# Out-projection issued group by group into a bank of its own, with two banks left for transposes and routing

## What is computed

```python
q = rope(einsum("bim,ghmd->bghid", x, w_aq)); k = rope(einsum("bim,gmd->bgid", x, w_ak))
v = einsum("bim,gmd->bgid", x, w_av)
s = einsum("bghid,bgjd->bghij", q * D**-0.25, k * D**-0.25) - 1e30 * (i < j)
o = einsum("bghij,bgjd->bghid", softmax(s), v)
r = einsum("bghid,ghdm->bim", o, w_ao)            # the out-projection
x1 = layernorm(x + r)
out = layernorm(x1 + routed_experts(x1) + shared_expert(x1))
```

## Time and profile before

| | us |
|---|---|
| median of 3 runs | 1107.93 |
| profiled execution, its own time | 1108.6 |
| its span, first to last instruction | 1106.8 |
| TensorE busy, share of the span | 1000.8 (90%) |
| VectorE | 654.8 (59%) |
| ScalarE | 523.8 (47%) |
| GpSimd | 370.4 (33%) |

### The profile page before, as it was taken

The page is one execution under the profiler, slowest core; times in us unless marked ns, Lnnn a source line. Parts: engine busy times, 40 slices in busy tenths (PEclk is TensorE's granted clock), DMA queues, the critical chain, the costliest instruction groups (busy, mean ns, idle before and its releaser), DMA issues.

```text
span 1106.8 us, 17288 instructions
## 1 busy us (share of the span) xinstructions
PE 1000.8 (90%) x5448; PEld 756.0 (68%) x5448; DVE 654.8 (59%) x1666; ACT 523.8 (47%) x1151; POOL 370.4 (33%) x407
## 2 busy tenths in 40 slices
PE   6999999699999999999998999999999998639826
PEld 4888887566778777777676666777777776526502
DVE  6777765366565576565655775564757647324408
ACT  4333334454564556464654555555655645116502
POOL 6666666223321212102134333212221120126722
PEclk9999999899999999999998999999999999859958
DMA  8455333533231212210223323432211123998697
GB/s 242 165 180 186 106 138 116 180 110 118 78 96 62 59 58 58 70 44 23 86 64 112 103 82 103 126 110 66 78 35 58 36 59 107 226 245 208 94 277 277
DMA packets 107417, 128.36 MB, mean 116 GB/s; under 512 B 16465, under 2 KB 73925, under 8 KB 107328
## 3 DMA queue, kind: packets, MB, share of 16 engines
q1 hardware_dynamic: 84688, 96.82, 28.4%
q10 hardware_dynamic: 13408, 22.09, 6.5%
q0 software_dynamic: 9232, 8.34, 4.2%
HBM read 81.99 MB, written 58.59 MB: 127 GB/s over the span
## 4 chain that ended last, share of the span: by engine, by line
PE 71%; DVE 12%; issue 6%; DMA 4%; ACT 2%; POOL 2%; SPq 1%; ACTq 0%; DVEq 0%; POOLq 0%
PE s_ps L1051 15%; PE o_ps L1078 11%; PE ring L1061 9%; PE ring L1090 9%; PE o_ps L1081 6%; PE s_ps L1022 5%; PE ring L1022 5%; DVE neg_max L1253 2%; PE s_ps L1144 2%; PE s_ps L1029 1%; PE s_ps L1054 1%; DVE fsum L1452 1%; PE ring L1105 1%; DVE pt_lo L1191 1%; ACT pt_hi L830 1%
## 5 line engine op out<-in xcount | busy, mean ns | idle before, releaser
L1253 DVE TENSOR_REDUCE neg_max<-s_ps 128x1 f32<-128x128 f32 (+7 forms) x256 | 191.7, 751 | 165.1 <-PE s_ps L1054 160.9
L1051 PE MATMUL s_ps<-kt,qt_hi 128*128 128x512 f32 (+3 forms) x768 | 243.9, 399 | 8.4 <-POOL qt_lo L776 6.1
L904 ACT ACTIVATE probs<-s_ps,neg_max 128x128 f32<-128x128 f32 (+7 forms) x256 | 189.4, 740 | 130.6 <-DVE neg_max L1253 122.9
L776 POOL TENSOR_TENSOR qt_lo<-q_raw,qt_hi 128x512 fp32r<-128x512 f32 x64 | 81.9, 1281 | 325.3 <-ACT qt_hi L830 325.1
L1061 PE MATMUL ring<-ident,probs 128*128 128x128 f32 x1152 | 176.8, 276 | 7.2 <-DVE pt_lo L1191 4.5
L1051 PEld LDWEIGHTS s_ps<-kt,qt_hi 128*128 128x128 f32 x768 | 139.3, 194 | 64.3 <-issue 37.9
L1078 PE MATMUL o_ps<-pt,v 128*128 128x512 f32 x336 | 174.0, 600 | 2.7 <-DVE ot L1272 2.6
L1061 PEld LDWEIGHTS ring<-ident,probs 128*128 128x128 f32 x1152 | 128.9, 142 | 38.4 <-issue 22.9
L913 ACT ACTIVATE pt<-ring 128x512 f32<-128x512 f32 x168 | 99.7, 595 | 98.2 <-PE ring L1061 90.8
L1051 PE MATMUL s_ps<-kt,qt_lo 128*128 128x512 f32 (+3 forms) x384 | 134.0, 349 | 0.0
L801 POOL DMA_INDIRECT slot_rows<-row,slot_u x96 | 94.9, 988 | 97.9 <-DVE slot_u L1376 75.8
(11 more groups left out here) (197 smaller groups left out, 1525.5 us busy)
## 6 DMA issues: line engine op xcount, KB each, us to landing
q_rows<-q_out SPq DMA_DIRECT2D x64, 256.0 KB, 2.0
q_raw<-q_rows ACTq DMA_DIRECT2D x64, 256.0 KB, 2.8
inv_row<-inverses SPq DMA_DIRECT2D x64, 256.0 KB
fsum<-sums SPq DMA_DIRECT2D x48, 256.0 KB, 8.6
sums<-blank SPq DMA_DIRECT2D x16, 640.0 KB, 4.9
wexp<-in_L_ffn_w_gate_dram SPq DMA_DIRECT2D x32, 192.0 KB, 5.4
wexp<-in_L_ffn_w_up_dram SPq DMA_DIRECT2D x32, 192.0 KB, 5.8
wexp<-in_L_ffn_w_down_dram SPq DMA_DIRECT2D x32, 192.0 KB, 7.1
```

What stands on the lines that cost most here:

```text
L904: act.activation(probs[:, u % 2, h, 0:blocks(u) * P], s_ps[:, n % 2, score_cols(n)], ACT.Exp, bias=neg_max[:, n % 8:n % 8 + 1], accum_out= ...
L1051: pe.matmul(s_ps[:, n % 2, c + a:c + e], q[qp], k[kp][:, a:e], start=(qp == kp == 0), stop=(qp == 1 and not last))
L1253: dve.tensor_reduce(neg_max[:, n % 8:n % 8 + 1], s_ps[:, n % 2, score_cols(n)], AX_X, ALU.max, negate=True).then_inc(max_ready, 1)
```

## The change

Outproj gets a bank of its own, the third of the ring, and the other ring steps take turns in the two that are left. The matmuls of group g are issued as soon as they can be: those of groups 0, 1 and 2 in new steps `outpart`, each after the first product (`pv(u, 0)`) of the next unit, those of group 3 in the old `outproj` step. They accumulate in the one bank over the tile. By the list of steps the new steps stand, in tiles with four or more key blocks, at heads 10, 14 and head 2 of the next tile; with three at 11, 15 and 3; with two at 13 and heads 1 and 5 of the next tile; with one at heads 1, 5 and 6 of the next tile. `fit` moves from head 3 to head 2 in tiles with i % 8 = 0.

```diff
-    (("fit",), -2, (3, 5, 5, 2)),
+    (("fit",), -2, (2, 5, 5, 2)),
...
         seq.append(("pv", u, j))
+        if j == 0 and u % G:
+            seq.append(("outpart", u - 1))
...
+        elif s[0] == "outproj":
+            r = PRE_BANKS + RING - 1
         elif s[0] in RINGED:
-            r = PRE_BANKS + n % RING
+            r = PRE_BANKS + n % (RING - 1)
             n += 1
...
-                if kind in PRE_RINGED + RINGED:
+                if kind in PRE_RINGED + RINGED and kind != "outproj":
                     begin(s)
...
-                if kind == "outproj":
-                    i = s[1]
-                    pe.wait_ge(wo_loaded, 16)
-                    for h in range(G * H):
-                        if h % H == 0:
-                            pe.wait_ge(o_ready, G * i + h // H + 1)
-                        ins = pe.matmul(bank(s)[:, 0:M], ot[:, h // H, (h % H) * P:(h % H + 1) * P], wo[:, h, :],
-                                        start=(h == 0), stop=(h == G * H - 1))
-                    ins.then_inc(attn_ready, 1)
+                if kind in ("outpart", "outproj"):
+                    u = s[1] if kind == "outpart" else G * s[1] + G - 1
+                    i, g = divmod(u, G)
+                    if g == 0:
+                        begin(("outproj", i))
+                        pe.wait_ge(wo_loaded, 16)
+                    pe.wait_ge(o_ready, u + 1)
+                    for h in range(H):
+                        ins = pe.matmul(bank(("outproj", i))[:, 0:M], ot[:, g, h * P:(h + 1) * P], wo[:, g * H + h, :],
+                                        start=(g == h == 0), stop=(g == G - 1 and h == H - 1))
+                    if g == G - 1:
+                        ins.then_inc(attn_ready, 1)
```

## The result

The changed kernel takes 1125.26 us (median of 4 runs, 1124.43 to 1126.50) against 1108.17 us; the ratio is 1.0152, 95% interval 1.0134 to 1.0169. The forecast was 1121 us, range 1109 to 1133; rival C's 1125 to 1131 us holds the measured time too. The profiled execution of the changed kernel took 1124.45 us, its span is 1121.8 us (1106.8 before): +15.0 us.

A forecast was written before the change was run, and what follows sets the result against it. TensorE's own work was taken to bound the full tiles. Losses of 6.4 and 12.5 us less a gain of 4.7 us gave +14.2 us, 1122 us, rounded down to 1121 us; range 1109 to 1133 us.

The forecast's parts named there:

- rival C: Short tiles 1, 2, 9 or 10: two or three more slow-clock stretches add 3.4 to 10 us, 1125 to 1131 us; chance 0.13.
- a piece covers the wait in tiles 1 and 9: Head 15: the bank is read out 1.4 us late, but a 1.77 us piece at head 13 covers it, so 0.
- Work moved, none saved: Out-projection: the same 512 matmuls, 7.07 us a tile before and after; no instruction changes engine, no DMA or queue entry moves.
- Loss 1: Outproj's last piece waits uncovered for group 3's scaled output at six places: 6.4 us, bounds 5 to 9 us.
- Loss 2: Transposes and routing get two banks, so TensorE waits for read-outs where VectorE is behind: 12.5 us, bounds 6 to 25 us.
- 15 to 20: Expected sign in the profile: transposes' waits for low halves and routing read-outs grow from some 6 us to 15 to 20.
- Rival A: Pieces at heads 10 to 15 relieve VectorE and ScalarE, so it ends not slower: 1107 us, or 1103 us; chance 0.14.
- Gain: Pieces fall into TensorE's holes, mainly tiles 1, 2, 8, 9 and 10, and save 4.7 us, bounds 3 to 8 us.
- The sum for the loop, +14.2 us: Attention loop: 6.4 us and 12.5 us lost less 4.7 us gained, added to the profiled execution.
- a sign of being wrong: TensorE's clock: the forecast would be wrong if the slow stretches of the clock changed; no size given.
- From the last outproj to the end the same 149 us: Last tile's routing, experts and final sum: untouched by the change, so this stretch stays at 149 us.
- The Trainium skill: Ring of banks: its rule of rotating matmul groups through banks makes a bank held open a loss; no figure, no term.

The follow-up runs named there:

- the banks alone: Against the kernel before: outproj has its own bank, other ring steps two, fit at head 2, but outproj stays in one block; 1120.3 us, ratio 1.0128.
- the repeat: The changed kernel measured once more, nothing altered; 1125.0 us, ratio 1.0149 to the kernel before.
- the two kernels with pick 0 moved: First part of the routing choice moved from head 11 to 12 in tiles with four or more key blocks: changed kernel 1115.3 us, kernel before 1104.1 us.

## Why the prediction was right, and where it was off

The forecast was +13 us and the measurement +17.1. The sign, the two losses and their order held; three steps did not: that nothing moves behind the last outproj, that a piece covers the wait in tiles 1 and 9, and that the clock stays as it was.

**Work moved, none saved: right.** L1096 has 512 matmul records of 379 ns, as before. Eight follow each other at the old spacing and a piece takes 1.7 us more on TensorE wherever it stands; the cut costs no starts that one can see.

**Loss 1, predicted 6.4 us: right, a little large.** Six waits as named, 5.0 us; tile 2 shows the form. The wait was 0.84 us in place of 1.0 to 1.2: DVE idled ahead of the scaling and began at once, which was the condition of the lower bound, 5 us.

```profile
251.19 0.69 DVE L1279 TENSOR_TENSOR ot<-o_ps,inv_row 128x512 f32<-128x512 f32 x1 [0.80 <-PE o_ps L1082]
251.94 1.35 PE L1096 MATMUL ring<-wo,ot 128*128 128x256 f32 x5 [0.84 <-DVE ot L1279]
```

**Loss 2, predicted 12.5 us: right in size for the banks alone (12.0 us), less in the changed kernel, and wrong in its places.** In the changed kernel the transposes wait 13.1 us in place of 6.8 ("15 to 20" was the sign named) and the matmul of ht 3.0 us, so 9.3 us more; without the 1.0 us of waits for L1362 and y_sb that the change took away it is 10.3 us for banks. In tile 5 the wait is 1.45 us where 0.59 us was, net 0.9 (1.14 predicted), in tile 6 1.67 for 0.61; tiles 7 and 15 lose 0.9 and 1.2 us net (0.8 predicted). In tiles 3, 4 and 8 I expected 0.7, 0.2 and 0.8 us and found none in the changed kernel: with the banks alone a transpose of tile 3 does wait 0.57 us and one of tile 8 0.63 us, so the pieces took these. In tiles 1 and 9 I expected none, and it was 1.3 us each. The step that failed is "a piece stands between and covers it":

```profile
231.35 1.89 PE L1096 MATMUL ring<-wo,ot 128*128 128x256 f32 x8
233.44 0.23 PE L1058 MATMUL s_ps<-causal_bf,ident_bf 128*128 128x128 bf16 x1
233.71 0.42 DVE L1260 TENSOR_REDUCE neg_max<-s_ps 128x1 f32<-128x256 f32 x1 [1.99 <-PE s_ps L1058]
...
235.12 0.26 DVE L1317 TENSOR_TENSOR hid<-ring,hid 128x96 f32<-128x96 f32 x1
...
235.43 0.66 PE L1065 MATMUL ring<-ident,probs 128*128 128x128 f32 x4 [1.28 <-DVE hid L1317]
```

The reader (L1317) stands in DVE's order behind the row maximum of head 14, and that head's scores stand behind the piece. DVE idled 1.99 us waiting for them. A piece covers a read-out only if nothing ahead of the read-out on its own engine comes from behind the piece. Rival A's relief in the full tiles may have failed for the same reason, but no run separates that.

**Gain, predicted 4.7 us: about right in sum, by luck in its parts.** From the waits' sum: 5.0 of loss 1 + 10.3 of banks less the 9.6 measured leaves 5.7 us. The 1.56 us wait of tile 1 is gone, so is the one for L1362. The count waits, worth 2.3 us in the forecast, shrank from 4.5 to 4.1 us only; products that no longer wait for L1272 (2.6 us before, 0.5 after) and for low halves (1.3 us before) made up for it.

**The sum for the loop, +14.2 us, was measured as +14.3 us, partly by luck.** Waits make 9.6 us of it, while my terms were meant as waits throughout. Up to 3.4 us more are the clock, which I had left to rival C and whose change I had named as a sign of being wrong. The granted clock of the changed kernel in two stretches:

```profile
585.00:592.00 7.00, 7.00 (x31) 5.82 (x30) 2.44 (x9) 3.05 (x12) 4.52 (x5) 0.51 0.64 191
950.20:953.70 3.50, 3.50 (x13) 2.94 (x13) 1.98 (x9) 1.19 (x2) 1.00 (x1) 0.51 0.00 0
```

The profile's clock shows 1.2 GHz for 13.6 us of the loop (6.8 before; 13.6 again in the repeat, none at all with the banks alone). A full TensorE loses half of that, an estimate, so the 6.8 us more cost 3.4 us at most; that is rival C's mechanism, with one more stretch where it asked for two or three. Over the twelve profiles the loop has 10.2 to 13.6 us at 1.2 GHz in the seven executions with a cut outproj and 0 to 10.2 us in the five with whole blocks throughout: a link between cut and clock is likely, but the two sets touch and it isn't shown. Some 1.3 us are left; TensorE's first matmuls after a wait run late (a group of four transposes takes 0.66 us after one, 0.60 us otherwise).

**"From the last outproj to the end the same 149 us": wrong.** The step said that no DMA and no queue entry moves. None moves in the list, but the sync queue's wait for the last product does, against everything behind it, and 2.4 us came of that in one profile of the changed kernel, 1.3 in the other. In the prediction this was a term at zero whose cover I had not named. It is a third to over half of the distance from the forecast; the other part is the rounding down from 1122 and the spread of the runs (1123.4 to 1126.5 over both sets).

**The Trainium skill** had the sign right: independent groups should rotate through the banks (Perfetto Trace Analysis, Optimizing Tensor Performance, Matmuls). The runs here put a number to it for this kernel: 12 us for one bank of three, and 6 of them, by the two kernels with pick 0 moved, at heads where one vector engine step of 2 us stood in the way.

## What to carry to other kernels

Splitting work on the engine that bounds the kernel saves nothing by itself; count instead what the old block covered (here 5.3 us ahead of a late operand, and a queue of loads that started on the last product) and what the split must pay with (here a bank). To price a smaller ring, take for each step the end of the read-out that would now have to be over, and count a cluster of negative spares once; then look at what stands ahead of those read-outs on the reading engine, because moving that may be worth nearly as much as the buffer (4 us with three banks, 10 us with two, against 12 for the bank). Check then whether the moved instruction has kept its length, or two causes are measured as one. A filler placed ahead of a wait helps only if the awaited engine isn't itself fed from behind the filler.

## What the runs showed of the hardware

An add of 64 columns on the vector engine (biased, L1318) took 1.33 us beside a GpSimd subtraction of 512 columns (the kernel before, tile 5):

```profile
407.02 1.30 POOL L776 TENSOR_TENSOR qt_lo<-q_raw,qt_hi 128x512 fp32r<-128x512 f32 x1 [8.19 <-ACT qt_hi L830]
407.07 1.33 DVE L1318 TENSOR_TENSOR biased<-sig,bias_sb 128x64 f32<-128x64 f32 x1
```

It ended with the GpSimd instruction, 0.08 us after it. Five of the 16 adds are of this kind in both kernels (1.31 to 1.33 us, tiles 5, 6, 7, 13 and 14). With pick 0 one head later (here the changed kernel with it) GpSimd is done before the add begins, and it takes 0.22 us in tile 5:

```profile
412.27 1.29 POOL L780 TENSOR_TENSOR qt_lo<-q_raw,qt_hi 128x512 fp32r<-128x512 f32 x1 [9.82 <-ACT qt_hi L834]
413.78 0.22 DVE L1325 TENSOR_TENSOR biased<-sig,bias_sb 128x64 f32<-128x64 f32 x1
```

So 1.1 of the 2 us of pick 0 were this meeting. The other thing I had not expected is the size of the scatter ahead of the loop: the same projections end up to 3.7 us apart between executions, with the clock at 1.2 GHz for longer or shorter stretches around 183 to 211 us.
